# Two attentions over 32 keys, written out as a pipeline of eight slots, with their masks added by TensorE

## The reference, cut to what matters

```python
x = x + _L0_xattn_ref(_layernorm(x), ctx_1024, ctx_1024, mask, Wq, Wk, Wv, Wo)      # l0x, cross
...
x = x + _L1_attn_ref(_layernorm(x), ln1_g, ln1_b, ..., Wqkv, Wo, W1, b1, W2, b2)    # l1a, self

# l0x: 16 heads of 8 features; 32 queries, 257 keys
scores = einsum('bhqd,bhkd->bhqk', qh, kh) / sqrt(8)
scores = where(key > query, -1e9, scores)      # causal
scores = where(mask == 0, -1e9, scores)        # mask of keys
out = einsum('bhqk,bhkd->bhqd', softmax(scores), vh) @ Wo.T

# l1a: 16 heads of 8 features; 32 queries, 32 keys; q and k are rotated by position
s = where(causal, rotate(q) @ rotate(k).T / sqrt(8), -inf)
x = x + (softmax(s) @ v) @ Wo                  # an MLP follows
```

## Time and profile before

| | |
|---|---|
| median of 3 runs | 4537.35 us (4535.98 to 4552.52) |
| the profiled execution | 4539.18 us, span 4537.4 us, mean granted clock 0.862 |
| PE busy | 3368.4 us, 74% |
| PEld / DVE / ACT / POOL busy | 2389.6 / 2767.4 / 2168.6 / 1600.4 us |
| l0x_sum, first load issued | 13.9 us |
| l0x_att, first load issued to last addition | 94.1 to 462.5 us |
| l1a_att, first load issued to last addition | 1732.3 to 1956.7 us |

### The profile page before, as it was taken

How to read it: one execution, slowest core, us unless ns; L and a number is a source line. 1 busy time by engine, 2 the same in 40 slices (tenths; PEclk the granted TensorE clock), 3 DMA queues, 4 the chain that set the end, 5 groups by cost and what they waited for, 6 DMA issues and landing times. The chain is left out here.

```text
span 4537.4 us, 88936 instructions
## 1 busy us (share of the span) xinstructions
PE 3368.4 (74%) x26727; PEld 2389.6 (53%) x26727; DVE 2767.4 (61%) x6307; ACT 2168.6 (48%) x6522; POOL 1600.4 (35%) x1340
## 2 busy tenths in 40 slices
PE   0677766578899985765779999778874274977966
PEld 0555663246677765744557777533333242753644
DVE  4777565635577766933357777589895511344872
ACT  1333442168677764432256666454552012554963
POOL 0211010000355655500535555288882061112840
PEclk9788786789999998986989999899996586887988
DMA  6000000022222210001201111144442021940000
GB/s 191 8 6 5 8 0 5 0 67 79 60 67 67 67 52 6 0 5 55 59 25 30 29 30 29 32 156 135 136 140 97 7 34 49 240 100 9 2 2 23
DMA packets 170075, 239.99 MB, mean 53 GB/s; under 512 B 60932, under 2 KB 132903, under 8 KB 167056
## 3 DMA queue, kind: packets, MB, share of 16 engines
q1 hardware_dynamic: 161768, 228.42, 17.2%
q0 software_dynamic: 8128, 9.45, 1.2%
HBM read 206.85 MB, written 14.11 MB: 49 GB/s over the span
## 5 line engine op out<-in xcount | busy, mean ns | idle before, releaser
L3083 PE MATMUL l2a_pY<-l2a_hc,ident 128*128 128x512 f32 x512 | 271.3, 668 | 93.3 <-POOL l2a_hc L3000 58.7
L2387 POOL TENSOR_TENSOR l2x_att_prob<-l2x_att_prob,l2x_att_rs 128x1028 f32<-128x1028 f32 x128 | 243.4, 1901 | 274.4 <-DVE l2x_att_rs L2572 274.4
L2531 ACT ACTIVATE l2x_att_prob<-l2x_att_pS,l2x_att_nmx 128x257 f32<-128x257 f32 x512 | 236.3, 474 | 208.9 <-DVE l2x_att_nmx L2567 208.9
L2387 POOL TENSOR_TENSOR l1x_att_prob<-l1x_att_prob,l1x_att_rs 128x1028 f32<-128x1028 f32 x128 | 243.4, 1901 | 206.2 <-DVE l1x_att_rs L2572 206.2
L2531 ACT ACTIVATE l1x_att_prob<-l1x_att_pS,l1x_att_nmx 128x257 f32<-128x257 f32 x512 | 236.3, 474 | 147.3 <-DVE l1x_att_nmx L2567 147.2
L2970 POOL TENSOR_TENSOR l2a_dbu<-l2a_dx,l2a_BC 128x1024 f32<-128x1024 f32 x128 | 298.6, 2354 | 21.1 <-PE l2a_pY L3083 10.7
L3100 ACT ACTIVATE l2a_pA<-l2a_dl,l2a_A 128x512 f32<-128x512 f32 x256 | 174.6, 689 | 188.0 <-DVE l2a_pH L3206 113.1
L2583 DVE COPY l1x_att_probT<-l1x_att_pT 86x512 f32<-86x512 f32 x256 | 175.4, 685 | 114.9 <-PE l1x_att_pT L2473 107.5
L2583 DVE COPY l2x_att_probT<-l2x_att_pT 86x512 f32<-86x512 f32 x256 | 175.7, 686 | 107.8 <-PE l2x_att_pT L2473 107.8
L3206 DVE TENSOR_TENSOR_SCAN l2a_pH<-l2a_pA,l2a_dbu 128x512 f32<-128x512 f32 x192 | 224.8, 1216 | 23.7 <-POOL l2a_dbu L2970 11.9
L3083 PEld LDWEIGHTS l2a_pY<-l2a_hc,ident 128*128 128x128 f32 x512 | 103.3, 210 | 252.9 <-issue 118.6
(11 more groups left out here) (720 smaller groups left out, 9548.4 us busy)
## 6 DMA issues: line engine op xcount, KB each, us to landing
l2a_BC<-l2a_rows SPq DMA_DIRECT2D x128, 512.0 KB, 3.7
l3x_att_ctn<-ctx_n SPq DMA_DIRECT2D x32, 576.0 KB, 13.5
l0x_sum_ctx<-ctx_t SPq DMA_DIRECT2D x16, 1028.0 KB, 4.8
l1x_k_xin<-ctx_t SPq DMA_DIRECT2D x32, 514.0 KB, 3.5
l1x_att_ctx<-ctx_t SPq DMA_DIRECT2D x128, 128.5 KB, 2.1
l1x_att_kT<-l1x_KA SPq DMA_DIRECT2D x128, 128.5 KB, 2.2
l2x_att_ctx<-ctx_t SPq DMA_DIRECT2D x128, 128.5 KB, 2.1
l3x_att_ctx<-ctx_t SPq DMA_DIRECT2D x32, 514.0 KB, 11.7
```

The source lines that it names most:

```text
L2387: pool.tensor_tensor(p, p, bc(rs[:, b, :], 2, KEYS), ALU.mult).then_inc(scaled, 1)
L2531: last = act.activation(prob[:, b, j, 0:KEYS], pS[:, j, 0:KEYS], ACT.Exp, bias=nmx[:, b, j:j + 1], accum_out=sums[:, b, j:j + 1])
L3083: last = pe.matmul(pY[c][:, :], env.ident[:, :], hc[:, u % 3, c, :], start=False, stop=n == NS - 1)
```

## The change

`context_tail_sum` is gone. In cross `block_attention` loads whole key rows (257) for each tile into three buffers `kvs`, and DVE sums the last 225 columns per tile (`tail_sum`).

The masks are numbers 0 and -1e30 in bf16 (`fill`: 32 rows for the causal one, written by ACT, in cross a 33rd row with the mask of keys, made by DVE on one partition). PE adds them in `scores` by one product of `pick_b` with `fill` over 512 columns, ahead of the four score products and summed with them in PSUM. In cross the subtraction takes the maximum with -1e9 in the same instruction. The factor of q goes into `wq` once.

`own_head` keeps only its product and writes it by head; `output` has four products with `wo`, one per head, summed in PSUM. `scale` moves from DVE to POOL, where it stands ahead of `keys`; DVE keeps `factors`. `own` has two buffers, `prob` three, `v` four.

The loops are written out: each engine's stream has the steps of all tiles, one behind the other, in a new order, with tile n between n + 3 (`project`) and n - 3 (`output`, `add`). What the diff leaves out are indices of buffers by n instead of s.

```diff
--- before.py
+++ after.py
...
-        context_tail_sum(nc, env, "l0x_sum", csum)
+    normalise(nc, env, "l0x_ln", env.X, dst_t=env.XNT)
+    block_attention(nc, env, "l0x_att", w, env.X, cross=True)
...
+        pick, causal = st.sb("pick", [S, S]), st.sb("causal", [S, S])
+        pick_b = st.sb("pick_b", [rows, 4, S], BF16)
+        fill = st.sb("fill", [rows, B if cross else BT * 4, S], BF16)
+        v = st.sb("v", [P, 4, BT, D])
+        prob, probT = st.sb("prob", [P, 3, BT * 4, S]), st.sb("probT", [P, 2, BT, P])
+        own = st.sb("own", [P, 2, 4, P])
...
-            kvs = st.sb("kvs", [P, 2, BT, S])
-            keep_i = st.sb("keep_i", [P, B, S], I32)
+            kvs = st.sb("kvs", [P, 3, BT, KEYS])
+            csum, cs = st.sb("csum", [P, 4, BT]), st.sb("cs", [P, 2, BT, 4])
+            mask_i, mask = st.sb("mask_i", [rows, B, S], I32), st.sb("mask", [rows, B, S])
-            loads += [(keep_i[:, :, :], env.a.mask_pad[:, 0:S].unsqueeze(0).to_broadcast([P, B, S])),
+            loads += [(mask_i[S:rows, :, :], env.a.mask_pad[:, 0:S].unsqueeze(0)),
...
             @block.gpsimd
-                def slot(n, s):
-                    if inside(n + 3):
-                        keys(n + 3, 1 - s)
-                run_slots(pool, slot, units, first=-3)
+                def scale(n):
+                    pool.wait_ge(rs_made, made(n))
+                    pool.tensor_tensor(prob[:, n % 3], prob[:, n % 3], bc(rs[:, n % 2, :], 2, S), ALU.mult
+                                       ).then_inc(p_scaled, 1)
+                for n in range(-2, units):
+                    if inside(n):
+                        scale(n)
+                    if inside(n + 2):
+                        keys(n + 2)
...
             @block.sync
+                    for n in range(units):
+                        after(sp, qk_made, n - 3)
+                        after(sp, xs_ready, n - 3)
+                        after(sp, cs_made, n - 3)
+                        sp.dma_start(kvs[:, n % 3].rearrange("p b k -> p (b k)"),
+                                     env.a.ctx_t[:, n * BT * KEYS:(n + 1) * BT * KEYS]).then_inc(landed[n % 3], 16)
...
             @block.tensor
+                def scores(n):
                     pe.wait_ge(kb_made, made(n))
                     after(pe, shifted, n - 2)
+                    if n == 0:
+                        pe.wait_ge(filled, 2 if cross else 1)
+                        pe.wait_ge(picked, 2 if cross else 1)
+                    masked = bc(fill[:, n * BT:(n + 1) * BT, :], 2, 4) if cross else fill[:, :, :]
+                    pe.matmul(pS[n % 2][:, :], pick_b[:, :, :].rearrange("r h q -> r (h q)"), masked, start=True,
+                              stop=False)
                     for b in range(BT):
-                        last = pe.matmul(pS[s][:, b * P:(b + 1) * P], qb[:, s, b].rearrange("p h q -> p (h q)"),
-                                         kb[:, s, b].rearrange("p j k -> p (j k)"))
+                        last = pe.matmul(pS[n % 2][:, b * P:(b + 1) * P], qb[:, n % 2, b].rearrange("p h q -> p (h q)"),
+                                         kb[:, n % 2, b].rearrange("p j k -> p (j k)"), start=False, stop=b == BT - 1)
                     last.then_inc(s_made, 1)
...
-                    pe.wait_ge(ot_made, made(n))
+                def output(n):
+                    pe.wait_ge(own_made, made(n))
                     after(pe, added, n - 1)
-                    pe.matmul(pX[:, 0:D], oT[:, s, :], wo[:, :]).then_inc(out_made, 1)
+                    for h in range(4):
+                        last = pe.matmul(pX[:, 0:D], own[:, n % 2, h, :], wo[:, :], start=h == 0, stop=h == 3)
+                    last.then_inc(out_made, 1)
+                for n in range(-3, units + 4):
                     if inside(n + 1):
-                        scores(n + 1, 1 - s)
-                    if inside(n):
-                        turn(n, s)
+                        scores(n + 1)
+                    if inside(n - 1):
+                        turn(n - 1)
+                    if inside(n - 2):
+                        attend(n - 2)
+                    if inside(n - 3):
+                        output(n - 3)
                     if inside(n + 3):
-                        project(n + 3, 1 - s)
+                        project(n + 3)
                     if inside(n + 2):
-                        project_values(n + 2, s)
-                    if inside(n):
-                        attend(n, s)
-                    if inside(n - 1):
-                        output(n - 1, 1 - s)
-                run_slots(pe, slot, units, first=-3)
+                        project_values(n + 2)
...
             @block.scalar
+                if cross:
+                    act.activation(wq[:, :], wq[:, :], ACT.Copy, scale=HD ** -0.5).then_inc(scaled, 1)
+                act.activation(fill[0:S, :, :], bc(causal[:, :], 1, B if cross else BT * 4), ACT.Copy
+                               ).then_inc(filled, 1)
...
+                for n in range(-2, units + 2):
+                    if inside(n + 1):
+                        values(n + 1)
+                    if inside(n + 2) and cross:
+                        projections(n + 2)
                     if inside(n + 2):
-                        stage_tokens(n + 2, s)
-                    if inside(n):
-                        keep_turned(n, s)
-                    if inside(n + 3):
-                        projections(n + 3, 1 - s)
+                        stage_tokens(n + 2)
+                    if inside(n - 1):
+                        keep_turned(n - 1)
                     if inside(n + 1):
-                        exponentials(n + 1, 1 - s)
-                    if inside(n + 1) and cross:
-                        stage_tail(n + 1, 1 - s)
-                    if inside(n + 2):
-                        values(n + 2, s)
-                run_slots(act, slot, units, first=-3)
+                        exponentials(n + 1)
+                    if inside(n) and cross:
+                        stage_tail(n)
...
             @block.vector
+                def tail_sum(n):
+                    dve.wait_ge(landed[n % 3], 16 * (n // 3 + 1))
+                    after(dve, cs_ready, n - 4)
+                    dve.tensor_reduce(csum[:, n % 4, :], kvs[:, n % 3, :, S:KEYS], AX.X, ALU.add).then_inc(cs_made, 1)
+                def scores(n):
                     dve.wait_ge(s_made, made(n))
+                    after(dve, p_made, n - 2)
+                    sc = pS[n % 2][:, :].rearrange("p (g k) -> p g k", k=S)
+                    m = mx[:, n % 2, :]
                     if cross:
-                        sc4 = pS[s][:, :].rearrange("p (b j k) -> p b j k", j=4, k=S)
-                        dve.tensor_tensor(sc4, sc4, bc(keep[:, bass.ds(n * BT, BT), :], 2, 4), ALU.mult
-                                          ).then_inc(kept, 1)
-                        dve.wait_ge(kept, made(n))
-                        dve.tensor_tensor(sc4, sc4, bc(fill[:, bass.ds(n * BT, BT), :], 2, 4), ALU.add
-                                          ).then_inc(score_step, 1)
-                    else:
-                        dve.tensor_tensor(sc, sc, bc(causal[:, :], 1, BT * 4), ALU.add).then_inc(score_step, 1)
-                    dve.wait_ge(score_step, made(n))
-                    after(dve, p_made, n - 2)
-                    dve.tensor_reduce(mx[:, s, :], sc, AX.X, ALU.max).then_inc(m_made, 1)
-                    if cross:
+                        dve.tensor_reduce(m, sc, AX.X, ALU.max).then_inc(m_made, 1)
                         dve.wait_ge(m_made, 2 * n + 2)
-                        dve.tensor_scalar(mx[:, s, :], mx[:, s, :], NEG, None, ALU.max).then_inc(m_made, 1)
+                        dve.tensor_scalar(m, m, NEG, None, ALU.max).then_inc(m_made, 1)
                         dve.wait_ge(m_made, 2 * n + 3)
                     else:
+                        dve.tensor_reduce(m, sc, AX.X, ALU.max).then_inc(m_made, 1)
                         dve.wait_ge(m_made, made(n))
-                    after(dve, t_made, n - 2)
-                    dve.tensor_tensor(prob[:, s], sc, bc(mx[:, s, :], 2, S), ALU.subtract).then_inc(shifted, 1)
-                def scale(n, s):
+                    after(dve, t_made, n - 3)
+                    if cross:
+                        dve.scalar_tensor_tensor(out=prob[:, n % 3], in0=sc, scalar=NEG, in1=bc(m, 2, S), op0=ALU.max,
+                                                 op1=ALU.subtract).then_inc(shifted, 1)
+                    else:
+                        dve.tensor_tensor(prob[:, n % 3], sc, bc(m, 2, S), ALU.subtract).then_inc(shifted, 1)
+                def factors(n):
                     dve.wait_ge(p_made, made(n))
...
-                    dve.reciprocal(rs[:, s, :], sums[:, s, :]).then_inc(rs_made, 1)
-                    dve.wait_ge(rs_made, made(n))
+                    after(dve, p_scaled, n - 2)
```

(79 more changed lines are left out.)

173 lines of the change are left out of this document (62 added, 111 removed).

## The result

The changed kernel took 4346.88 us (median of 4 runs, 4340.6 to 4353.34), the kernel before 4537.9 (4 runs). The ratio is 0.957, with a 95% interval of 0.9545 to 0.96. The profiled execution has a span of 4351.2 us against 4537.4: 186.2 us less.

The account below looks back on a forecast made before the run. No engine bounds the whole span; VectorE bounds self, a PE-DVE wait loop cross. 60.1 + 15.5 + 118 - 4 - 1 - 3 = 185.6, taken as 186 to 188, off 4539.2 gives 4351 us; range 4300 to 4420.

Parts of the forecast that it names:

- the outer stage's closing: End of the outer stage: raised the summed gain of 185.6 us to 186 to 188.
- Tail-sum stage: Stage ahead of cross: removing it gains 60.1 us; its sum returns as 1.02 us a tile on DVE.
- Prologue: Start of cross: 11.7 us gained in loads and 3.8 before the first scores, together 15.5.
- Cross slots: Cross loop: PE becomes the bound at clock 1.00, 10.21 to 6.4 us a slot, 118 us gained.
- The first slots: Start of the cross loop: some 4 us lost at low clock.
- Drain: End of cross: 1 us lost to a longer drain.
- Self: Self loop: a new one-slot cycle through rotate, keys and scores, 6.4 us against 6.31, 3 us lost.
- The lock: Cross, DVE and POOL excluding each other: L1775 meets `scale` and waits some 0.35 us, already in its mean.
- The rival: Cross: three small DVE instructions each wait for a full POOL instruction, 8.4 us a slot, 4413 us; 9%.
- The clock: Cross rival: a fifth of PE's work stays at 1.2 GHz, slot 7.6 us, 4388 us; 9%.
- Written-out loops: Rival, both stages: straight instruction stream starves an engine, slower than before, 4607 us at 4 us a slot; 3%.
- The first rival: Self: the cycle does not bind, slot falls to PE's 5.35 us, 33 us more gained, 4318 us; 12%.

Follow-up runs that it names:

- e8: Kernel before with only the tail-sum stage removed: cross loads whole keys and sums tails in VectorE's slot; 4475.83 against 4532.17 us, ratio 0.9879.
- e1: Changed kernel with rotate moved ahead of factors and scores in VectorE's slot of the self stage; 4319.58 us, ratio 0.9478 to the kernel before.
- e5: Changed kernel with the sum over heads back on VectorE in both stages and one output product; 4359.93 us, ratio 0.9575 to the kernel before.
- e7: Kernel before with the slots of its two block attentions written out instead of looped; 4564.44 against 4557.99 us, ratio 1.0018.
- a1: Kernel before, unchanged, profiled on the chip of the other runs; 4531.02 us (one run).

## Why the prediction was right

It forecast 4351 and the median is 4346.88. By the profiled executions the cross side ends 197.4 us sooner (last addition ended at 462.5, now at 265.17), self takes 8.1 longer, and the parts that the change doesn't touch differ by +3.1: 186.2. The mechanism was right in both stages. That the sum (185.6 forecast, 186.2 measured) fits to 1 us is luck: prologue, drain and loop came out 8 us better, self and the rest 8 us worse, and within the cross loop 11 us of longer steady slots met 13 us of shorter first ones. The up to 2 us that the prediction adds for the outer stage's closing have no row behind them, and nothing in the runs shows them.

- *Tail-sum stage.* Norm 74.41 to 13.47, 60.9 gained, forecast 60.1. The sum costs 1.08 us a tile, forecast 1.02. e8 tests the part by itself.
- *Prologue.* First load to first scores on DVE 14.7 us (33.14 to 47.8) instead of 32.6 (94.06 to 126.7): 18.0 gained, forecast 15.5. `fill` took 3.60 (3.8); the loads landed in 6.1 us, not 8.0.
- *Cross slots: right mechanism, PE's sum too small.* The loop did get bound by PE, at clock 1.00 and 50.00 of 50 busy, but the steady slot is 6.74 to 6.75, not 6.36. Going by starts, the mask product takes 0.31 (0.25 forecast), the tail product 1.05 (1.02), the small products pE 0.53 (0.44), and scores and values 1.00 and 0.98, where 0.89 was taken for both. `attend` and the four output products together took 1.89, as forecast. Why four scores take 1.00 here, and 0.89 in the earlier trace rows before the same transposes, no run shows. The first slots cancelled that: 4.20, 4.56, 5.16, 5.35 and 6.06 between DVE's first maxima, for PE has fewer groups in them. I had counted 4 us against them; they gave some 9. Loop: 116.1 gained, forecast 118 - 4.
- *Drain.* 2.4 us shorter (16.9 from the last tile's first score instruction on DVE to the last addition, 19.2 before), forecast 1 longer. 1.4 of it are the two mask passes, which stood there too.
- *Self.* The cycle was the forecast, 6.4 us against 6.57 measured, and e1 shows it by opening it. Step by step: rotation's end to POOL 0.08, POOL 2.85, to PE 0.05, mask product to DVE's maximum 1.51, DVE 2.08. The term that was too small is PE's: the mask product moved the scores by 0.31 (0.25 forecast) and the scores' record is 1.16 long (1.06), which together make up the difference, for the handovers took 0.17 of the 0.2 laid out. The stage loses 8.1 us, not 3: 31 x (6.63 - 6.31) = 10 in the loop, where two first slots of 7.26 and 7.10 count too, less 2 before and behind it.
- *The lock.* L1743, the maximum with -1e9, 0.17 alone, waits for a POOL instruction in every steady slot. It was forecast to meet `scale`; it starts 0.01 us behind `qb`, the product after that. From the groups by shape, 100 to 150 us, and one slot's timeline:

```profile
L1743 DVE TENSOR_SCALAR l0x_att_mx<-l0x_att_mx 128x16 f32<-128x16 f32 x8 | 8.5, 1061 | 0.3
...
148.08 1.04 POOL L1532 TENSOR_TENSOR l0x_att_qb<-l0x_att_qk,m 128x512 f32<-128x512 f32 x1
148.09 1.06 DVE L1743 TENSOR_SCALAR l0x_att_mx<-l0x_att_mx 128x16 f32<-128x16 f32 x1
```

 That is 0.9 us a slot, where 0.35 was laid out. It cost nothing, for DVE (46.74 of 50) still stayed under PE. The rival was wrong in price: one of the three instructions meets POOL, not all (the other two took 0.18 us each). In e5, where DVE is the fullest, the same instruction starts 0.77 us into `scale`, near the place that the prediction laid out (0.85), takes 0.31, and the slot is 6.63.
- *The rivals.* The clock stayed at 1.00. (In self it did so with a wait of PE of 0.87 us in every slot, so a wait in each round did not by itself bring it down, though the prediction's wording of that rule says so.) Written-out loops starve no engine: e7 shows no new idle put down to issue; its self stage is 18 us longer by the lock's new order and its cross loop 5 us shorter, and the whole, 6 to 8 us longer, does not resolve these 13, since the unedited parts differ by more from one execution to the next. (The Trainium skill, "Runtime: NRT & Kernel Launch", section "Instruction fetch mechanics", has straight code fetched ahead; e7 agrees, with 82.7 us of idle put down to issue against 87.1.) The first rival, self at PE's 5.35, was wrong for this kernel and right for e1 (5.41).

What stays open: what in the loop gives DVE its lead of 0.05 to 0.06 us in the kernel before; why the first cross slot differs (4.20 and 3.84 us in two executions of the changed kernel); why a group of four products takes 0.89 in one place and 1.00 in another; and what the masks on TensorE are worth by themselves.

## What to carry to other kernels

When an order of instructions is rewritten, draw the cycle that each engine's queue closes and count the slots it spans; here the change left a one-slot cycle of 6.57 us in a stage whose fullest engine needs 5.4, and one moved call was worth 44 us, nearly a quarter of what the whole change gained. Price TensorE by start-to-start times of whole slots, not by the sum of single groups. Work moved between two engines that are both nearly full (the head sum) was worth nothing here, and work taken off an engine that doesn't bind (the scaling, in cross) neither. What paid was removing a stage (61 us), most of a prologue (18), a wait between engines by the new order (56 of the loop's 116, net of the tail sum) and taking masks, scaling and head sum off VectorE together (the other 60).

## What the runs showed of the hardware

- Where a VectorE and a GpSimd instruction exclude each other, a lead of 0.03 to 0.06 us repeats in every steady slot and decides who pays: 6.31 or 7.07 us a slot for the same instructions (a1, e7).
- An instruction of VectorE over 16 elements in each of 128 partitions, 0.17 us long alone, can wait 0.9 us for a GpSimd product in each slot (1.06 us, when it started 0.01 us behind it).
- Four fp32 products of 128x128x128 move the next group's start by 0.89 to 1.00 us, and the two groups' kinds alone don't decide which: scores before transposes took 0.89 in one slot of before and 1.00 in the changed kernel, `attend` before the output products 1.00 in cross and 0.89 in self.
